# In an 8x8-state scan, TensorE adds ub to the second state by an identity product accumulated in its bank, and VectorE's order per step is changed

## The chip, the cores and the metric

One Trainium2 chip, one core. The metric is the device time in microseconds (us) of one execution, given as the median of several runs. The kernel runs a whole small network in one launch: a recurrent mixing layer with a time scan, followed by six layers of windowed attention and feed-forward. Only the scan is touched here.

## The reference, cut to what matters

```python
def step(s, inp):                      # s: one 8x8 state for each batch row and head
    q_, w_, k_, v_, a_, b_ = inp
    sa = jnp.einsum('bhij,bhj->bhi', s, a_)
    s = s * w_[:, :, None, :] + sa[..., None] * b_[:, :, None, :] + v_[..., None] * k_[:, :, None, :]
    return (s, jnp.einsum('bhij,bhj->bhi', s, q_))
s0 = jnp.zeros((Bx, H, HS, HS), x.dtype)       # H = 16 heads, HS = 8
_, y = jax.lax.scan(step, s0, (qt, wt, kt, vt, at, bt))      # B = 2, T = 1024
...
x = _layernorm(x + mixing(x));  x = _layernorm(x + six_layers(x))
```

Every token multiplies the state with `a`, sums over a head's 8 columns (`sa`), adds `sa * b` and `v * k`, and reads the state with `q`.

## The kernel before, in words

The 2 x 1024 tokens are cut into 64 chunks of 32 tokens, and all chunks run at once: a step `l` of the scan (`CHUNK` = 32 of them, l = 0 to 31) handles token l of every chunk. Since a chunk does not know its starting state, two states are carried. State 0 begins at zero and collects what the chunk adds (`v*k`). State 1 begins as the identity matrix and becomes the matrix that carries a starting state through the chunk. Each is a 128 x 512 fp32 tile in a PSUM bank of its own: `S_BANKS[0]` is bank 4, `S_BANKS[1]` is bank 5. Decays are folded into the step vectors, so a step only adds to a state. After the scan a serial chain over the 32 chunks of a sequence (`chain` on TensorE, `next_start` on VectorE) finds the starting states, then come the outputs of the mixing layer and the six layers (the "stream").

One step of the scan, for states p = 0 and 1:

- VectorE `times_a(p, l)` (L666): `m[p]` = state p times `a`.
- TensorE `product_u(p, l)` (L924): a product with `headones`, which sums over a head's rows, into `U_BANKS[p]`. A 128 x 512 fp32 product stands in the trace as two passes.
- VectorE `times_b(p, l)` (L671): `ub[p]` = that sum times `b`.
- State 1: VectorE `renew1(l)` (L684) adds `ub[1]` to bank 5 in place.
- State 0: GpSimd `add_vk(l)` (L845) makes `ubvk` = `ub[0]` + `vk`, and VectorE `renew0(l)` (L677) adds that to bank 4 in place.
- Reading: VectorE `times_r(l)` (L691) multiplies state 1 with `r`; ScalarE `copy_state(l)` (L514) copies bank 4 to SBUF and GpSimd `times_r(l)` (L852) multiplies the copy. TensorE `products_y(l)` (L932), 8 products of 128 columns in 16 passes, gathers both.
- GpSimd `times_k(l + 2)` (L838) prepares `vk` two steps ahead, from the tile `v_rep` that SyncE's copies (L453, 16 DMAs for 8 steps) fill.

Beside that, in steps 0 to 23, `in_step` inserts the making of the next group's step vectors: on VectorE two more instructions in the steps with l % 8 = 2, 3 and 4 and one with 5, 6 and 7 ("stages"); on TensorE `sums_of_squares` (L917) at l = 0, 8 and 16. TensorE also runs `product_rk` (L945) at l = 25 to 28.

The order on each engine is written out by hand, and every engine runs its own list in order. Per step TensorE's list is: `product_u(1, l+1)`, `product_u(0, l+1)`, `products_y(l-1)`, then `sums_of_squares` or `product_rk` if there is one. VectorE's is the loop at L732.

After the last step VectorE makes the first part of what the chain needs: `end_g` (L709, reads state 1), `spread_g_first` (L716), `make_prop` (L725), then `renew0(31)`, `times_r(31)`, `end_h` (L730) and two memsets (L752), on which the chain's first product waits.

Of the kernel before, what the change touches and what calls it, by code (L numbers as in the profile page):

```python
# [24 lines left out]
ALU = mybir.AluOpType  # L25
# [3 lines left out]
P = 128  # L29
B, T, C = 2, 1024, 128  # L30
N = B * T
HEADS, HS = 16, 8
GROUP = 512
GROUPS = N // GROUP
CHUNK = 32
CHUNKS = N // CHUNK
# [302 lines left out]
def build_steps(nc, a, sems, ctx, t, banks, v_dram, v_rep, state, y, zy, x_mid, x):  # L339


    def sig(name, **kw):
        return Signal(sems, name, **kw)

    def sb(name, shape):
        return ctx.enter_context(nc.sbuf_tensor(name, shape, F32))
# [9 lines left out]
    m, ub = sb("sc_m", [P, 2, W]), sb("sc_ub", [P, 2, W])  # L356
# [12 lines left out]
    s_set = sig("s_set")  # L369
    s_new = [sig(f"s_new{p}") for p in range(2)]  # L370
    s_a = [sig(f"s_a{p}") for p in range(2)]
    u_product = [sig(f"u_product{p}") for p in range(2)]
    ub_made = [sig(f"ub_made{p}") for p in range(2)]
    s_copied, y_product, y_read, ended = sig("s_copied"), sig("y_product"), sig("y_read", per=2), sig("scan_ended")
    s_r = [sig(f"s_r{p}") for p in range(2)]
# [8 lines left out]
    start = spare[:, CHUNKS * QUAD:CHUNKS * (QUAD + HS)].rearrange("p (c r) -> p c r", r=HS)  # L384
# [14 lines left out]
    U_BANKS, Y_BANKS, S_BANKS = (banks[0], banks[1]), (banks[2], banks[3]), (banks[4], banks[5])  # L399
# [7 lines left out]
    def step(tile, l):  # L407

        return tile[:, CHUNKS * l:CHUNKS * (l + 1)].unsqueeze(1).to_broadcast([P, HS, CHUNKS])

    def rows(ap):
        return ap.rearrange("p (r c) -> p r c", c=CHUNKS)
# [24 lines left out]
    def vk_of(l):  # L437
        return vk[(l // STEPS) % 2][:, :, l % STEPS, :]

    def in_step(l, stages):  # L440

        j, s = (l + STEPS) // STEPS, l % STEPS
        if j < GROUPS:
            for stage in stages[s]:
                stage(j)
# [158 lines left out]
    def vector(dve):  # L604
# [1 line left out]
        nc.vector.tensor_scalar(bonus_ones[:, :], t["headones"][:, :], vecs[:, V_FAAAA:V_FAAAA + 1], None, ALU.mult).then_inc(constants_made.sem, 1)  # L606
        nc.vector.scalar_tensor_tensor(out=head_centring[:, :], in0=t["headones"][:, :], scalar=-1.0 / HS, in1=t["ident"][:, :],
                                       op0=ALU.mult, op1=ALU.add).then_inc(constants_made.sem, 1)
        nc.vector.tensor_copy(rows(S_BANKS[1][:, :]), t["rowmask"][:, :].unsqueeze(2).to_broadcast([P, HS, CHUNKS])).then_inc(s_set.sem, 1)

        def soft_sum(j):
            dve.wait_ge(z_log.sem, j + 1)
# [44 lines left out]
        def times_a(p, l):  # L657

            if l:
                dve.wait_ge(s_new[p].sem, l)  # L660
            else:
                dve.wait_ge(s_set.sem, 1)
            if l >= 2 - p:
                dve.wait_ge(u_product[p].sem, l + p - 1)
            dve.wait_ge(a_made.sem, l // STEPS + 1)
            nc.vector.tensor_tensor(rows(m[:, p, :]), rows(S_BANKS[p][:, :]), step(a_step, l), ALU.mult).then_inc(s_a[p].sem, 1)  # L666

        def times_b(p, l):
            dve.wait_ge(u_product[p].sem, l + p)
            dve.wait_ge(b_made.sem, l // STEPS + 1)  # L670
            nc.vector.tensor_tensor(rows(ub[:, p, :]), rows(U_BANKS[p][:, :]), step(b_step, l), ALU.mult).then_inc(ub_made[p].sem, 1)  # L671

        def renew0(l):
            if l:
                dve.wait_ge(vk_added.sem, l + 1)
                dve.wait_ge(s_copied.sem, l)
                nc.vector.tensor_tensor(S_BANKS[0][:, :], S_BANKS[0][:, :], ubvk[:, :], ALU.add).then_inc(s_new[0].sem, 1)  # L677
            else:
                dve.wait_ge(vk_made.sem, 1)
                nc.vector.tensor_copy(rows(S_BANKS[0][:, :]), vk_of(0)).then_inc(s_new[0].sem, 1)  # L680

        def renew1(l):
            dve.wait_ge(ub_made[1].sem, l + 1)
            nc.vector.tensor_tensor(S_BANKS[1][:, :], S_BANKS[1][:, :], ub[:, 1, :], ALU.add).then_inc(s_new[1].sem, 1)  # L684

        def times_r(l):
            dve.wait_ge(s_new[1].sem, l + 1)
            dve.wait_ge(r_made.sem, l // STEPS + 1)
            if l >= 2:
                dve.wait_ge(y_product.sem, y_product.after(l - 2))  # L690
            nc.vector.tensor_tensor(m2[:, l % 2, :, 1, :], rows(S_BANKS[1][:, :]), step(r_step, l), ALU.mult).then_inc(s_r[1].sem, 1)  # L691
# [14 lines left out]
        def end_g():  # L706
            dve.wait_ge(s_new[1].sem, CHUNK)
            dve.wait_ge(ub_made[0].sem, CHUNK - 1)
            nc.vector.tensor_tensor(rows(G_BANK[:, :]), rows(S_BANKS[1][:, :]), last, ALU.mult).then_inc(g_set.sem, 1)  # L709
# [17 lines left out]
        def end_h():  # L727
            dve.wait_ge(s_copied.sem, CHUNK)
            dve.wait_ge(s_new[0].sem, CHUNK)
            nc.vector.tensor_tensor(rows(state[:, 0, :]), rows(S_BANKS[0][:, :]), last, ALU.mult).then_inc(ended.sem, 1)  # L730

        for l in range(CHUNK):  # L732
            if l:
                times_b(0, l)
            times_b(1, l)
            renew1(l)
            if l + 1 < CHUNK:
                times_a(1, l + 1)
            else:
                end_g()  # L740
                for s in range(B):
                    spread_g_first(s)
                for s in range(B):
                    make_prop(0, s)
            renew0(l)
            if l + 1 < CHUNK:
                times_a(0, l + 1)
            times_r(l)
            in_step(l, stages)
        end_h()  # L750
        for s in range(B):
            nc.vector.memset(start[:, SEQ_CHUNKS * s, :], 0.0).then_inc(start_set.sem, 1)  # L752
# [157 lines left out]
    def tensor(pe):  # L910

        def sums_of_squares(j):
            pe.wait_ge(squared.sem, j + 1)
            if j:
                pe.wait_ge(a_made.sem, j)
                pe.wait_ge(kk_gated.sem, j)
            nc.tensor.matmul(KK_BANK[:, :], t["headones"][:, :], sq[:, :], start=True, stop=True).then_inc(ss_product.sem, 1)  # L917

        def product_u(p, l):

            pe.wait_ge(s_a[p].sem, l + p)
            if l >= 2 - p:
                pe.wait_ge(ub_made[p].sem, l + p - 1)
            nc.tensor.matmul(U_BANKS[p][:, :], t["headones"][:, :], m[:, p, :], start=True, stop=True).then_inc(u_product[p].sem, 1)  # L924
# [11 lines left out]
        def product_rk(j):  # L936

            pe.wait_ge(rk_made.sem, j + 1)
            pe.wait_ge(constants_made.sem, 2)
            if j < 2:  # L940
                pe.wait_ge(r_made.sem, GROUPS)
                pe.wait_ge(kk_gated.sem, GROUPS)
            else:
                pe.wait_ge(rk_read.sem, j - 1)
            nc.tensor.matmul(RK_BANKS[j % 2][:, :], bonus_ones[:, :], rk[:, g_of[j]], start=True, stop=True).then_inc(rk_product.sem, 1)  # L945

        sums_of_squares(0)
        product_u(1, 0)
        stages = ((sums_of_squares,), (), (), (), (), (), (), ())
        for l in range(CHUNK):  # L950
            if l + 1 < CHUNK:
                product_u(1, l + 1)
                product_u(0, l + 1)
            if l:
                products_y(l - 1)
            in_step(l, stages)
            if l >= CHUNK - STEPS + 1 and l < CHUNK - STEPS + 1 + GROUPS:
                product_rk(l - (CHUNK - STEPS + 1))
# [1129 lines left out]
```

## Time and profile before

| | us |
|---|---|
| three runs | 1924.15, 1926.08, 1927.91 |
| median | 1926.08 |
| span of the profiled execution, first to last instruction | 1924.9 |
| scan in it, from the first `times_b` (L671) to the memset that lets the chain begin (L752) | 79.47 to 256.37 |

All times below are those of the profiled execution, counted from its first instruction. Its span is 1.2 us below the median of the runs. PE is the matmul row of TensorE and PEld its weight loads, DVE is VectorE, ACT is ScalarE, POOL is GpSimd. Neighbouring records of one kind are merged into one row with an "x" count; a record starts when its waits are over.

### The profile page before, as it was taken

The page shows a single profiled execution, that of the slowest core. Times are in us where ns is not written, and L with a number is a line of the kernel's source. Part 1 is how long each engine was busy: PE and PEld are TensorE (multiplying, and loading weights), DVE is VectorE, ACT ScalarE, POOL GpSimd, SP SyncE. Part 2 cuts the span into 40 slices and gives each one's busy share as a digit, 9 for nine tenths or more (in the row PEclk, how much of TensorE's full clock was granted, in tenths as well). Part 3 has the DMA queues.
Part 4 walks back from the last instruction along what each step waited for, and adds up shares of the span by engine and source line. Part 5 has one row for each costly group of instructions (what it writes and reads, how often), then busy time and mean ns, then how long its engine had stood idle before and what let it go on. Part 6 is the DMA issues. An engine that isn't in the chain of part 4 may idle for free.

```text
span 1924.9 us, 72907 instructions
## 1 busy us (share of the span) xinstructions
PE 1751.1 (91%) x31158; PEld 1185.3 (62%) x31158; DVE 1550.0 (81%) x2150; ACT 1138.0 (59%) x2221; POOL 1259.8 (65%) x981
## 2 busy tenths in 40 slices
PE   7577876899999989999899999899998999999985
PEld 2144553466666666667666767666666676666663
DVE  6599957788888878888888888788887888888853
ACT  5523223557676747676667676667675667676742
POOL 3476743777777767777667777677776777777730
PEclk9699977999999989999999999999998999999986
DMA  4534201222222232222322222322223222222220
GB/s 97 127 53 51 29 3 70 58 67 70 69 73 68 72 104 79 63 75 70 112 66 79 69 73 83 103 62 77 69 72 109 69 68 79 63 76 67 70 61 26
DMA packets 68257, 137.27 MB, mean 71 GB/s; under 512 B 17952, under 2 KB 23520, under 8 KB 66912
## 3 DMA queue, kind: packets, MB, share of 16 engines
q1 hardware_dynamic: 67936, 132.62, 27.0%
q8 instruction: 246, 4.03, 0.9%
q14 instruction: 75, 0.61, 0.1%
HBM read 29.79 MB, written 2.10 MB: 17 GB/s over the span
## 4 chain that ended last, share of the span: by engine, by line
PE 40%; DVE 22%; issue 11%; POOL 9%; DMA 7%; ACT 4%; SPq 2%; DVEq 0%; ACTq 0%; POOLq 0%
PE bank L1460 9%; PE bank L1370 6%; PE bank L1443 6%; POOL rot L1308 5%; DMA v_shift<-v_tok 5%; DVE rot L1770 5%; PE bank L1418 5%; PE bank L1501 3%; PE bank L1375 3%; PE bank L1477 3%; DVE total L1796 2%; DVE rnorm L1776 2%; POOL probs L1332 2%; DVE probs L1789 2%; DMA p_T<-p_blocks 1%
## 5 line engine op out<-in xcount | busy, mean ns | idle before, releaser
L1770 DVE TENSOR_TENSOR rot<-bank,gains 128x1024 f32<-128x1024 f32 x384 | 462.3, 1206 | 158.8 <-ACT squares L1603 142.8
L1314 POOL TENSOR_TENSOR rot<-rot,rnorm 128x1024 f32<-128x1024 f32 x192 | 361.0, 1901 | 319.3 <-ACT rnorm L1613 317.1
L1308 POOL TENSOR_TENSOR rot<-rot 128x512 f32<-128x512 f32 x384 | 480.6, 1274 | 6.9 <-DVE rot L1770 6.9
L1370 PE MATMUL bank<-wqkv,x 128*128 128x512 f32 x768 | 404.9, 612 | 10.5 <-issue 5.0
L1603 ACT ACTIVATE squares<-bank 128x512 f32<-128x512 f32 x384 | 232.8, 606 | 256.5 <-PE bank L1370 255.9
L1332 POOL TENSOR_TENSOR probs<-probs,total 128x1024 f32<-128x1024 f32 x96 | 182.7, 1903 | 125.3 <-DVE total L1798 125.3
L1644 ACT ACTIVATE o_T<-bank 128x512 f32<-128x512 f32 x192 | 104.2, 598 | 254.2 <-PE bank L1443 254.2
L1776 DVE TENSOR_REDUCE rnorm<-squares 128x16 f32<-128x1024 f32 x192 | 233.0, 1214 | 2.8
L1443 PE MATMUL bank<-p_T,v_shift 64*64 64x32 f32 x6144 | 194.7, 223 | 26.6 <-DMA p_T<-p_blocks 21.9
L1443 PEld LDWEIGHTS bank<-p_T,v_shift 64*64 64x64 f32 x6144 | 169.2, 138 | 79.1 <-issue 49.6
L1383 PEld LDWEIGHTS bank<-st_ident,rot 128*128 128x128 f32 x1536 | 179.9, 143 | 59.9 <-issue 53.6
L1375 PE MATMUL bank<-wqkv,x 128*128 128x512 f32 x384 | 206.6, 621 | 2.7 <-DVE rot L1770 2.7
L1443 PE MATMUL bank<-p_T,v_tok 64*64 64x32 f32 x6144 | 193.3, 222 | 4.4 <-issue 4.4
L1383 PE MATMUL bank<-st_ident,rot 128*128 128x128 f32 x1536 | 194.0, 275 | 0.0
L1460 PE MATMUL bank<-o_T,wo 128*128 128x256 f32 x768 | 176.9, 384 | 0.0
L1443 PEld LDWEIGHTS bank<-p_T,v_tok 64*64 64x64 f32 x6144 | 170.5, 139 | 5.5 <-issue 5.4
L1477 PE MATMUL bank<-xn_T,w 128*128 128x256 f32 (+1 forms) x576 | 164.5, 395 | 9.2 <-ACT gate_T L1670 2.2
L1460 PEld LDWEIGHTS bank<-o_T,wo 128*128 128x128 f32 x768 | 146.4, 192 | 42.9 <-issue 22.4
L1418 PE MATMUL bank<-k_T,q_T 64*32 64x64 f32 x12288 | 161.8, 225 | 11.8 <-issue 10.3
L1418 PEld LDWEIGHTS bank<-k_T,q_T 64*32 64x32 f32 x12288 | 140.8, 105 | 39.2 <-issue 33.1
L1477 PEld LDWEIGHTS bank<-xn_T,w 128*128 128x128 f32 (+1 forms) x576 | 97.7, 182 | 99.2 <-DVE ff_T L1822 45.5
L1370 PEld LDWEIGHTS bank<-wqkv,x 128*128 128x128 f32 x768 | 131.6, 191 | 39.1 <-issue 16.2
(196 smaller groups left out, 2849.2 us busy)
## 6 DMA issues: line engine op xcount, KB each, us to landing
p_T<-p_blocks SPq DMA_DIRECT2D x768, 64.0 KB
v_shift<-v_tok SPq DMA_DIRECT2D x96, 384.0 KB, 3.5
v_shift<-v_tok SPq DMA_DIRECT2D x96, 128.0 KB, 3.4
wqkv<-in_wqkv SPq DMA_DIRECT2D x6, 1536.0 KB, 8.0
v_rep_sb<-v_by_step SPq DMA_DIRECT2D x32, 128.0 KB
v_rep<-v_by_step SPq DMA_DIRECT2D x32, 128.0 KB
wo<-in_wo SPq DMA_DIRECT2D x6, 512.0 KB, 8.6
w<-in_w SPq DMA_DIRECT2D x6, 341.0 KB, 8.8
```

The source lines that it names most:

```text
L1308: nc.gpsimd.tensor_tensor(out=out, in0=out, in1=by_head(turned[:, part])[:, :, frm], op=ALU.add).then_inc(rot_added.sem, 1)
L1314: nc.gpsimd.tensor_tensor(out=by_head(qk[u][:, half]), in0=by_head(qk[u][:, half]), in1=rnorm[u][:, AH * i:AH * (i + 1)].unsqueeze(2).to_b ...
L1370: nc.tensor.matmul(QK_BANKS[i][:, :], shifted_tokens(x, n, P), layer_cols(wqkv, n, 3 * INNER, 512 * i, 512), start=True, stop=True).then_i ...
L1375: nc.tensor.matmul(V_BANKS[i][:, :], shifted_tokens(x, n, P), layer_cols(wqkv, n, 3 * INNER, 2 * INNER + 512 * i, 512), start=True, stop=T ...
L1383: mm = nc.tensor.transpose(outs[i // 4][:, P * (i % 4):P * (i % 4 + 1)], source[:, P * i:P * (i + 1)], ident[:, :])
L1418: mm = nc.tensor.matmul(s_banks(n)[p][at:at + WINDOW, 2 * WINDOW * a_:2 * WINDOW * (a_ + 1)], q_T[rows, a_, at:at + WINDOW], k_T[rows, a_, ...
L1443: mm = nc.tensor.matmul(o_banks(n)[g][DH * p:DH * (p + 1), at:at + WINDOW], v[rows, DH * head:DH * (head + 1)], p_T[n % 2][rows, turn_, he ...
L1460: mm = nc.tensor.matmul(ff_bank(m)[:, 0:PT], layer_cols(wo, n, INNER, C * i, C), o_T[:, i, :], start=(i == 0), stop=(i == PAIRS - 1))
L1477: mm = nc.tensor.matmul(ff_bank(m)[0:size, PT * j:PT * (j + 1)], layer_cols(w1, PAIR * m, 2 * FF, at + f0, size), xn_T[:, :], start=True, ...
L1603: nc.scalar.activation(squares[:, 512 * i:512 * (i + 1)], QK_BANKS[i][:, :], ACT.Square).then_inc(squared.sem, 1)
L1770: nc.vector.tensor_tensor(both, src.unsqueeze(1).to_broadcast([P, 2, 8, DH]), pair_of_gains.unsqueeze(2).to_broadcast([P, 2, 8, DH]), ALU. ...
L1776: nc.vector.reduce_sum(rnorm[n % 2][:, AH * h:AH * (h + 1)], by_head(squares[:, INNER * h:INNER * (h + 1)]), AX).then_inc(ss_made.sem, 1)
```

## The change

Four things change, all in the scan:

1. `renew1` leaves VectorE. TensorE does it with an identity product (`t["ident"]`, moving operand `ub[1]`) that accumulates in bank 5 (`start=False`). It stands first in TensorE's list of the step and waits for `ub[1]` of its step and for VectorE's `times_r(l-1)`, which reads the bank.
2. The initial state 1, an identity pattern that VectorE copied into the bank (L609), is put there by TensorE too, by an identity product of the row mask (`set_state`).
3. VectorE's order: `times_r` of a step moves behind `times_b(0)` of the next one, and state 0 is renewed and multiplied before state 1 is.
4. TensorE's `product_u(0)` now stands before `product_u(1)`.

```diff
-        nc.vector.tensor_copy(rows(S_BANKS[1][:, :]), t["rowmask"][:, :].unsqueeze(2).to_broadcast([P, HS, CHUNKS])).then_inc(s_set.sem, 1)
...
-        def renew1(l):
-            dve.wait_ge(ub_made[1].sem, l + 1)
-            nc.vector.tensor_tensor(S_BANKS[1][:, :], S_BANKS[1][:, :], ub[:, 1, :], ALU.add).then_inc(s_new[1].sem, 1)
...
         for l in range(CHUNK):
             if l:
                 times_b(0, l)
+                times_r(l - 1)
             times_b(1, l)
-            renew1(l)
+            renew0(l)
             if l + 1 < CHUNK:
+                times_a(0, l + 1)
                 times_a(1, l + 1)
             else:
                 end_g()
...
                 for s in range(B):
                     make_prop(0, s)
-            renew0(l)
-            if l + 1 < CHUNK:
-                times_a(0, l + 1)
-            times_r(l)
             in_step(l, stages)
+        times_r(CHUNK - 1)
         end_h()
...
+        def set_state():
+            nc.tensor.matmul(rows(S_BANKS[1][:, :]), t["ident"][:, :], t["rowmask"][:, :].unsqueeze(2).to_broadcast([P, HS, CHUNKS]),
+                             start=True, stop=False, skip_group_check=True).then_inc(s_set.sem, 1)
+
+        def renew1(l):
+            pe.wait_ge(ub_made[1].sem, l + 1)
+            if l:
+                pe.wait_ge(s_r[1].sem, l)
+            nc.tensor.matmul(S_BANKS[1][:, :], t["ident"][:, :], ub[:, 1, :], start=False, stop=True,
+                             skip_group_check=True).then_inc(s_new[1].sem, 1)
...
+        set_state()
         sums_of_squares(0)
         product_u(1, 0)
         stages = ((sums_of_squares,), (), (), (), (), (), (), ())
         for l in range(CHUNK):
+            renew1(l)
             if l + 1 < CHUNK:
+                product_u(0, l + 1)
                 product_u(1, l + 1)
-                product_u(0, l + 1)
             if l:
                 products_y(l - 1)
             in_step(l, stages)
```

VectorE's instructions of one step without stages, before (banks 0 and 1 hold the head sums of states 0 and 1; `s_new`, `ub_made`, `u_product` are raised by the renewals, `times_b` and `product_u`):

```order
L671 TENSOR_TENSOR sc_ub<-bank0,mk_sb 128x512 [waits b_step_made,u_product0]
L671 TENSOR_TENSOR sc_ub<-bank1,mk_sb 128x512 [waits b_step_made,u_product1]
L684 TENSOR_TENSOR bank5<-bank5,sc_ub 128x512 [waits ub_made1]
L666 TENSOR_TENSOR sc_m<-bank5,z_sb 128x512 [waits a_step_made,u_product1,s_new1]
L677 TENSOR_TENSOR bank4<-bank4,sc_ubvk 128x512 [waits s_copied,vk_added]
L666 TENSOR_TENSOR sc_m<-bank4,z_sb 128x512 [waits a_step_made,u_product0,s_new0]
L691 TENSOR_TENSOR sc_m2<-bank5,r_sb 128x8x64 [waits y_product,r_step_made,s_new1]
```

The same step of the changed kernel (its line numbers are 1 to 5 lower on VectorE):

```order
L670 TENSOR_TENSOR sc_ub<-bank0,mk_sb 128x512 [waits b_step_made,u_product0]
L686 TENSOR_TENSOR sc_m2<-bank5,r_sb 128x8x64 [waits y_product,r_step_made,s_new1]
L670 TENSOR_TENSOR sc_ub<-bank1,mk_sb 128x512 [waits b_step_made,u_product1]
L676 TENSOR_TENSOR bank4<-bank4,sc_ubvk 128x512 [waits s_copied,vk_added]
L665 TENSOR_TENSOR sc_m<-bank4,z_sb 128x512 [waits a_step_made,u_product0,s_new0]
L665 TENSOR_TENSOR sc_m<-bank5,z_sb 128x512 [waits a_step_made,u_product1,s_new1]
```

Seven instructions have become six: L684 is gone, the renewal of bank 4 follows at once on the second `times_b`, and `times_r` (of the step before) stands between the two `times_b`.

TensorE's list of one step, before:

```order
L924 MATMUL bank<-sc_m,headones_sb 128x512 [waits ub_made1,s_a1]
L924 MATMUL bank<-sc_m,headones_sb 128x512 [waits ub_made0,s_a0]
L932 MATMUL bank<-sc_m,collect_sb 128x128 [waits y_read,s_r1,s_r0]
L932 MATMUL bank<-sc_m,collect_sb 128x128 x7
```

And in the changed kernel, where `s_r1` is raised by VectorE's `times_r`:

```order
L921 MATMUL bank<-sc_ub,ident_sb 128x512 [waits s_r1,ub_made1]
L929 MATMUL bank<-sc_m,headones_sb 128x512 [waits ub_made0,s_a0]
L929 MATMUL bank<-sc_m,headones_sb 128x512 [waits ub_made1,s_a1]
L937 MATMUL bank<-sc_m,collect_sb 128x128 [waits y_read,s_r1,s_r0]
L937 MATMUL bank<-sc_m,collect_sb 128x128 x7
```

The renewal is a third 512-column product per step, ahead of the two others and behind the `products_y` of the step before.

## Rows read from the trace of the kernel before

**Rows 1.** The page, first part: busy us, share of the span, number of instructions
```profile
PE 1751.1 (91%) x31158; PEld 1185.3 (62%) x31158; DVE 1550.0 (81%) x2150; ACT 1138.0 (59%) x2221; POOL 1259.8 (65%) x981
```

**Rows 2.** Stretches: length, busy us per engine, granted TensorE clock, DMA share, GB/s
```profile
80.00:92.00 12.00, 8.35 (x13) 3.34 (x14) 8.27 (x14) 5.25 (x9) 5.00 (x4) 0.64 0.61 120
92.00:257.00 165.00, 128.02 (x639) 80.05 (x638) 153.97 (x245) 44.35 (x124) 115.34 (x94) 0.99 0.31 41
202.00:205.00 3.00, 3.00 (x15) 2.70 (x14) 2.41 (x5) 0.60 (x1) 1.69 (x2) 0.54 0.22 90
```

**Rows 3.** Timeline, all engines, one step: start, us, engine, line, operation [idle before <-releaser]
```profile
216.53 0.69 DVE L666 TENSOR_TENSOR sc_m<-bank,z_sb 128x512 f32<-128x512 f32 x1
217.14 0.68 DVE L691 TENSOR_TENSOR sc_m<-bank,r_sb 128x512 f32<-128x512 f32 x1
...
217.28 1.12 PE L924 MATMUL bank<-sc_m,headones_sb 128*128 128x512 f32 x2 [0.21 <-DVE sc_m L666]
...
218.24 1.95 PE L932 MATMUL bank<-sc_m,collect_sb 128*128 128x128 f32 x16
218.44 1.29 DVE L671 TENSOR_TENSOR sc_ub<-bank,mk_sb 128x512 f32<-128x512 f32 x2 [0.62 <-PE bank L924]
219.21 1.27 POOL L845 TENSOR_TENSOR sc_ubvk<-sc_ub,v_rep 128x512 f32<-128x512 f32 x1 [1.58 <-DVE sc_ub L671]
219.77 0.70 DVE L684 TENSOR_TENSOR bank<-bank,sc_ub 128x512 f32<-128x512 f32 x1
220.44 1.26 POOL L852 TENSOR_TENSOR sc_m<-sc_copy,r_sb 128x512 f32<-128x512 f32 x1
220.50 0.69 DVE L666 TENSOR_TENSOR sc_m<-bank,z_sb 128x512 f32<-128x512 f32 x1
221.11 0.69 DVE L677 TENSOR_TENSOR bank<-bank,sc_ubvk 128x512 f32<-128x512 f32 x1
221.67 1.27 POOL L838 TENSOR_TENSOR v_rep<-v_rep,k_sb 128x512 f32<-128x512 f32 x1
221.83 0.69 DVE L666 TENSOR_TENSOR sc_m<-bank,z_sb 128x512 f32<-128x512 f32 x1
```

**Rows 4.** Timeline, the next step: the gather and a 512-column product behind it
```profile
223.54 1.95 PE L932 MATMUL bank<-sc_m,collect_sb 128*128 128x128 f32 x16
223.74 1.29 DVE L671 TENSOR_TENSOR sc_ub<-bank,mk_sb 128x512 f32<-128x512 f32 x2 [0.62 <-PE bank L924]
225.33 1.02 PE L945 MATMUL bank<-kkraw_sb,bonus_ones 128*128 128x512 f32 x2
```

**Rows 5.** Chain that ended last, two steps with two stages each: start, us, what
```profile
147.14 1.29 DVE sc_ub L671 x2
152.92 1.29 DVE sc_ub L671 x2
```

**Rows 6.** Timeline, the scan's first steps
```profile
81.66 3.78 PE L924 MATMUL bank<-sc_m,headones_sb 128*128 128x512 f32 x4 [3.89 <-DVE sc_m L666]
91.73 1.29 DVE L671 TENSOR_TENSOR sc_ub<-bank,mk_sb 128x512 f32<-128x512 f32 x2 [1.57 <-PE bank L924]
```

**Rows 7.** Timeline, the last step and the start of the chain
```profile
250.24 1.29 DVE L671 TENSOR_TENSOR sc_ub<-bank,mk_sb 128x512 f32<-128x512 f32 x2 [0.62 <-PE bank L924]
...
252.24 1.26 POOL L852 TENSOR_TENSOR sc_m<-sc_copy,r_sb 128x512 f32<-128x512 f32 x1
252.30 0.70 DVE L709 TENSOR_TENSOR bank<-bank,decay 128x512 f32<-128x512 f32 x1
...
253.56 2.05 PE L932 MATMUL bank<-sc_m,collect_sb 128*128 128x128 f32 x16 [1.57 <-POOL sc_m L852]
...
256.37 0.08 DVE L752 MEMSET v_rep_sb<- 128x8 f32 x2
```

**Rows 8.** Timeline: the last copies into v_rep are issued, and GpSimd's first use of them
```profile
165.58 5.98 SPq L453 DMA_DIRECT2D v_rep<-v_by_step  x16
205.76 1.27 POOL L838 TENSOR_TENSOR v_rep<-v_rep,k_sb 128x512 f32<-128x512 f32 x1
```

## The prediction

> **What bounds the kernel now.** The page says PE 91%, DVE 81% [rows 1], but that is an average over stages; the change lives in the scan alone, so I read the scan by itself. From 92 to 257 us DVE is busy 153.97 of 165 us (93%), PE 128.02, POOL 115.34 [rows 2]: VectorE is the engine to look at. The timeline of one step without stages [rows 3, 4] shows why. `times_b(0)` starts at 218.44 and again at 223.74: a period of 5.30. In it VectorE runs seven instructions. One that does not need the one ahead starts 0.61 behind it (216.53 to 217.14), one that does 0.72 (221.11 to 221.83). The only gap is 0.62, ended by TensorE's L924. So before, a step is VectorE's seven instructions plus that short wait. Other steps: with two stages 5.78 (147.14 to 152.92) [rows 5], nine of them; one stage fits into the gap, so those nine take 5.30. The 29 periods from the `times_b(0)` at 91.73 to that of the last step at 250.24 are 158.5 us [rows 6, 7]; 9 x 5.78 + 20 x 5.30 = 158.0 agrees. Whatever leaves the scan leaves the total, since chain and stream follow serially.
>
> **Prices of what is added and moved.** All from [rows 3, 4, 7]. A 512-column product from standstill starts 0.06 after the VectorE instruction that releases it (216.53 + 0.69 to 217.28), takes 1.12 until its result and VectorE goes on 0.04 later (218.44); the array is free for the next work 0.96 after its start (218.24). With its weights loaded beforehand it takes 1.02 and occupies 0.86: the product at 225.33, straight behind a gather. The gather occupies 225.33 - 223.54 = 1.79. GpSimd's `add_vk` starts 0.77 after `times_b(0)` and takes 1.27; POOL releases another engine 0.06 after its end (252.24 + 1.26 to 253.56), and I take 0.05. GpSimd's three instructions need 3 x 1.23 = 3.7 per step.
>
> **The new step.** Set `times_b(0)` at 0. VectorE: `times_r` 0.61, `times_b(1)` 1.22. `renew0` could start at 1.94, but `ubvk` is ready at 0.77 + 1.27 + 0.05 = 2.09: the removed instruction uncovers a wait for GpSimd of 0.15 to 0.26. `times_a(0)` 2.81, its end 3.50, product 3.56, result and next `times_b(0)` at 3.56 + 1.12 + 0.04 = **4.72**. This is loop A, through VectorE, GpSimd, VectorE and TensorE.
> Loop B runs through TensorE's own list. From the array's start on `product_u(1)`: +0.86 the gather, +1.79 = 2.65 the identity product, +1.02 + 0.04 = 3.71 `times_a(1)`, +0.69 + 0.06 + 0.10 (weights) = **4.56**. B is 0.16 shorter than A, so A sets the step at 4.72 against 5.30. `times_a(1)` then starts near 3.5, when `times_a(0)` lets it go anyway (3.42): the identity product has next to no slack. That moving `renew1` costs the path nothing rests on this cover; whatever comes on top of it is paid once the 0.16 is used up.
>
> **The sum over the scan.**
> - Nine steps with one stage: the stage falls into VectorE's gap from 4.1 to 4.72. 9 x (4.72 - 5.30) = -5.2.
> - Nine with two: VectorE runs without a gap, 3.42 + 3 x 0.61 = 5.25. 9 x (5.25 - 5.78) = -4.8.
> - Five plain ones (l = 8, 16, 24, 25, 30): -2.9.
> - Where `sums_of_squares` stands behind the gather, the identity product starts 0.86 later, `times_a(1)` at 4.37, and `product_u(0)` is pushed too: the step takes 5.2 (l = 9, 17), -0.2, and passes 0.3 on to the next one each, +0.6.
> - `product_rk` in four successive steps: the first 5.2, then loop B with 0.86 more, 5.42, three times: -0.1 + 0.4 = +0.3. Here the new kernel is slower than the old one.
> - Start: TensorE is at the lower of its two levels for much of 80 to 92 us (granted 0.64), a product pair taking some 1.9 (3.78 for two) [rows 2, 6]. In step 0 `renew1` is on TensorE at that price, but the two head sums now begin early; I get `times_b(0)` of step 2 at 89.0 instead of 91.73, then a step of 6.9 if the clock is low for a stretch of it, as the granted share for 80 to 92 has it: 1.6 more than its 5.25. Net -1.1.
> - One stretch of 3.4 us at the lower level near 202 [rows 2] cost the old kernel 0.4, hidden mostly; with TensorE in both loops it costs 1.4: +1.0.
> - End: `end_g` waits for TensorE's last renewal, at 3.51 after `times_b(0)` instead of 2.06 (252.30 - 250.24); `renew0` has left the list behind it (-0.6). The memset that lets the chain begin comes at 6.9 to 7.0 instead of 6.13 (256.37 - 250.24) [rows 7]: +0.8.
> - `set_state` runs at the start while ScalarE works toward the first `sums_of_squares`; the VectorE copy that it replaces stood in a wait for ScalarE. Nothing either way, at most 0.1.
> - SyncE's queue: the last copies into `v_rep` are issued at 165.58, and GpSimd wants them at 205.76 [rows 8]. Both move with the scan, but the seven steps between are 3.3 us shorter. The copies' end is not shown by a row to the tenth, only that traffic is low from 202 on (share 0.22) [rows 2]. So 0 to 1.5 us of wait on GpSimd, which has 1.0 of slack per step; I take 0.
> Sum -5.2 - 4.8 - 2.9 - 0.2 + 0.6 + 0.3 - 1.1 + 1.0 + 0.8 = **-11.5 us**. From the profiled span of 1924.9 that is 1913.4; with the 1.2 us by which the median stands above it, 1926.1 - 11.5 = **1914.6**.
>
> **What is not in the trace of before: an accumulating identity product and a weight load behind a fresh wait.** Accumulation: seven of a gather's eight products accumulate, and 1.79 / 16 = 0.112 a pass gives no sign of a price; the lower bound is 0, the upper one rival 3's. The weight load: at 225.33 it was hidden under the gather, at 217.28 it was exposed (1.12 against 1.02). In a plain step `ub[1]` is ready at 1.96, the array free at 2.45, so I take it hidden; exposed, it costs 0.10 at the head of loop B in every step without cover and the sum falls to -9.4.
> The Trainium skill, "TensorE: Matmul & The Clock Gate", in its part on the architectural detail, says that TensorE pulls weight loads ahead of running matmuls. By that rule the load is hidden as I take it; by the exposed row the total would be 1916.7.
>
> **Rivals.**
> 1. *The result of the identity product is late* (exposed weights, a slower turn between TensorE and VectorE, GpSimd's sum coming later). Loop B has 0.16 of slack in plain steps, some 0.5 in two-stage ones, none in the `product_rk` steps. Walking the steps with 0.2 us more gives -7.9, with 0.4 -3.6, and the gain is gone at 0.57. Against it: every latency is from rows of the same engines. Time 1918 to 1922.5.
> 2. *TensorE's clock.* Between 80 and 92 us and near 202 us the low level struck the old kernel although TensorE was working [rows 2]. If the busier TensorE escapes both stretches, 1.6 and 1.0 to 1.4 come back: -14.3, 1911.8. The Trainium skill, the same page, Part 1 on the warmup, says that the throttled state is the default and that activity releases it; by that rule this is the outcome. The trace speaks half against it: the low stretch at 202 came in dense work. If instead further low stretches come, each costs 1.7 us.
> 3. *The other side: accumulating into a bank that another engine reads and that already holds data runs at half rate at 512 columns.* Then the identity product occupies 1.71, loop B is 4.56 + 0.85 = 5.41 in plain steps against 5.30, and 6.27 in `product_rk` steps. Over the scan I get +11: 1937. It is slower than before from about 0.57 us of additional time per product. Against it speaks the gather's pitch of 0.112 per accumulating pass; for it only that no 512-column product accumulates in this scan.
> 4. *Nothing gained:* VectorE's freed 0.7 us is replaced by waits of the same size, so that the step stays near 5.2. It takes the same 0.4 to 0.6 us as in rival 1: 1922 to 1930.
>
> **How the numbers follow.** Forecast -8 to -14 (1912 to 1918): 0.70. Rival 1, 1918 to 1922.2: 0.11. Rival 2, 1910 to 1912: 0.07. Rival 4 within 0.2%: 0.06. Rival 3 and the slow end of 4: 0.06. A change of 0.2% (3.9 us) is about what a measurement of this kernel can tell from none. So faster 0.88, same 0.06, slower 0.06. The range 1910 to 1921 holds the forecast, rival 2 and most of rival 1.
>
> **What would show it.** Right: `times_b(0)` to `times_b(0)` 4.7 in plain and one-stage steps, 5.25 in two-stage, 5.4 in three of the `product_rk` steps; VectorE waiting 0.15 to 0.26 for GpSimd's `add_vk` before each `renew0` of a plain step; PE pairs of 1.02 straight behind the gather; `end_g` 3.5 behind its step's `times_b(0)`. Wrong: a step above 4.9 with VectorE idle before `times_a(1)`, or PE idle between the gather and the identity product; a gap on GpSimd before `times_k(24)`. The forecast fails if loop B, not A, sets the plain step, or if the clock is low for more than two stretches of the scan.

## The result, and the profile after

| us | kernel before | changed kernel |
|---|---|---|
| median of the runs of the comparison | 1925.12 (4 runs) | 1905.55 (1897.81 to 1908.25, 4 runs) |
| span of the profiled execution | 1924.9 | 1906.3 |
| scan in it, first `times_b` to the memset ahead of the chain | 176.9 | 161.6 |
| from that memset to the end | 1668.5 | 1665.2 |

The ratio is 0.9896, 95% interval [0.9871, 0.9921]. One later execution of the kernel before took 4243 us, more than twice as long as any other, and is left out of every figure. Forecast were 1914.6 and a range of 1910 to 1921: faster, as said, but by some 20 us and not by 11.5. The time lies below the range. Two different things were missed, and the table shows both: the scan lost 15.3 us, and behind the scan, where nothing was changed, time went as well: 3.3 us in this pair of executions, 5.6 as a mean over many (below).

First the step. The timeline of the changed kernel, one plain step, answers to [rows 3, 4] (start, duration, engine, line and operation, idle before it and what ended that):

```profile
200.70 0.70 DVE L676 TENSOR_TENSOR bank<-bank,sc_ubvk 128x512 f32<-128x512 f32 x1 [0.18 <-POOL sc_ubvk L839]
200.96 0.30 PEld L921 LDWEIGHTS bank<-sc_ub,ident_sb 128*128 128x128 f32 x2
201.07 1.02 PE L921 MATMUL bank<-sc_ub,ident_sb 128*128 128x512 f32 x2
201.43 1.39 DVE L665 TENSOR_TENSOR sc_m<-bank,z_sb 128x512 f32<-128x512 f32 x2
202.18 1.98 PE L929 MATMUL bank<-sc_m,headones_sb 128*128 128x512 f32 x4
203.34 0.69 DVE L670 TENSOR_TENSOR sc_ub<-bank,mk_sb 128x512 f32<-128x512 f32 x1 [0.52 <-PE bank L929]
203.95 0.68 DVE L686 TENSOR_TENSOR sc_m<-bank,r_sb 128x512 f32<-128x512 f32 x1
204.00 1.95 PE L937 MATMUL bank<-sc_m,collect_sb 128*128 128x128 f32 x16
204.11 1.28 POOL L839 TENSOR_TENSOR sc_ubvk<-sc_ub,v_rep 128x512 f32<-128x512 f32 x1 [0.98 <-DVE sc_ub L670]
204.55 0.68 DVE L670 TENSOR_TENSOR sc_ub<-bank,mk_sb 128x512 f32<-128x512 f32 x1
205.42 0.70 DVE L676 TENSOR_TENSOR bank<-bank,sc_ubvk 128x512 f32<-128x512 f32 x1 [0.20 <-POOL sc_ubvk L839]
205.68 0.30 PEld L921 LDWEIGHTS bank<-sc_ub,ident_sb 128*128 128x128 f32 x2
205.78 1.02 PE L921 MATMUL bank<-sc_ub,ident_sb 128*128 128x512 f32 x2
```

From L676 to L676 it is 205.42 - 200.70 = 4.72, the forecast period. `add_vk` starts 0.77 after `times_b(0)` (203.34, 204.11), `renew0` waits 0.20 for it, and the identity product takes 1.02, its weights loaded beforehand (PEld 205.68, PE 205.78). The two `times_a` are one row of 1.39, where two instructions that wait for nothing take 1.29 (218.44 in [rows 3]). So `times_a(1)` is held for 0.10 by the identity product, whose result is there at 201.07 + 1.02 = 202.09, and starts 3.5 behind `times_b(0)`, as forecast. That costs the step nothing, since on TensorE `product_u(1)` stands behind `product_u(0)` anyway (202.18, both in one row of 1.98).

Then TensorE's clock and load by stretches. The rows of windows give: stretch, its length, then busy us of PE, PEld, DVE, ACT and POOL with their instruction counts, granted clock, DMA share, GB/s. The changed kernel, from 80 us to the end of its scan:

```profile
80.00:92.00 12.00, 11.61 (x32) 5.40 (x32) 8.98 (x15) 5.14 (x9) 7.43 (x6) 0.78 0.61 116
92.00:241.00 149.00, 142.01 (x667) 86.97 (x666) 131.85 (x208) 44.30 (x124) 112.63 (x92) 1.00 0.33 45
```

Against [rows 2] the clock is higher in the first stretch (0.78 for 0.64), and from 92 us on it is 1.00: no stretch at the lower level at all. The forecast had two such stretches in it.

The waits of VectorE between 84 and 242 us (what waited, for what: us in total, times, longest):

```profile
DVE sc_m L665 <- PE bank L921: 6.3, 9, 1.1
DVE bank L676 <- POOL sc_ubvk L839: 5.8, 30, 0.2
DVE sc_ub L670 <- PE bank L929: 5.3, 14, 1.0
```

Thirty times 0.2 for GpSimd, as forecast. For the identity product VectorE shows nine waits of its own, all in the steps that also hold a `sums_of_squares` or a `product_rk` or follow on one.

### The profile page after: what moved, and what is told of

It is laid out like the page before. It is cut to its first block, busy times and chain, and to the rows that moved or that the text cites. A ratio compares the mean times of both kernels' runs of the same rounds, so it can differ in the third digit from the quotient of the medians.

```text
span 1906.3 us, 73037 instructions
## 1 busy us (share of the span) xinstructions
PE 1774.9 (93%) x31224; PEld 1201.0 (63%) x31224; DVE 1527.7 (80%) x2117; ACT 1138.3 (60%) x2221; POOL 1260.5 (66%) x981
## 4 chain that ended last, share of the span: by engine, by line
PE 42%; DVE 16%; POOL 10%; issue 10%; DMA 10%; ACT 4%; SPq 4%; DVEq 0%; POOLq 0%; ACTq 0%
PE bank L1467 9%; PE bank L1450 7%; PE bank L1377 6%; POOL rot L1315 5%; DMA v_shift<-v_tok 5%; DVE rot L1777 5%; PE bank L1425 5%; PE bank L1382 3%; PE bank L1508 3%; PE bank L1484 3%; DVE rnorm L1783 2%; DVE total L1803 2%; POOL probs L1339 2%; DVE probs L1796 2%; PE bank L1390 2%
## 5 line engine op out<-in xcount | busy, mean ns | idle before, releaser
L1450 PE MATMUL bank<-p_T,v_shift 64*64 64x32 f32 x6144 | 197.9, 225 | 31.9 <-DMA p_T<-p_blocks 31.6
```

The lines of the kernel that those rows point to most:

```text
L1450: mm = nc.tensor.matmul(o_banks(n)[g][DH * p:DH * (p + 1), at:at + WINDOW], v[rows, DH * head:DH * (head + 1)], p_T[n % 2][rows, turn_, he ...
```

## Experiments

`times_b(0)` to `times_b(0)` is the period of a step. "Behind" is the time from the memset ahead of the chain to the end; where it is called a mean, it is the mean span of all runs of a kernel less the scan of its trace and less 79.4 us for what stands ahead of the scan (78.3 to 79.6 in the traces), and the value of before beside it is that of the runs taken together with them. The low time is the time in an execution at TensorE's lower level (1.2 GHz), worked out from the mean granted clock that each run has.

### The changed kernel again

> The changed kernel once more, for more times and a second profile. Theory: its gain is the scan's, 15 to 16 us from the first times_b to the memset before the chain (161.6 us after, 176.9 before), and what stands behind the scan differs between runs by several us either way through the granted clock. So the scan part reads 161 to 164 us, the part behind it lies anywhere in 1660 to 1672, and the ratio over five rounds settles near 1 - 15.3/1925 = 0.992 (0.990 to 0.994). Rival: the change also shortens what follows the scan, by some 5 us in every run; then the ratio stays at 0.9895 or lower and the part behind the scan reads below 1665 again.

Measured: 1906.70 (6 runs), ratio 0.9903 [0.9879, 0.9928]; behind, 1663.8 as a mean against 1667.4 of before (18 runs). Scan 162.6, one us more than in the first trace. Its timeline shows why, in the step at 113.44:

```profile
114.04 1.28 POOL L832 TENSOR_TENSOR v_rep<-v_rep,k_sb 128x512 f32<-128x512 f32 x1 [2.05 <-DMA v_rep<-v_by_step]
115.26 1.28 POOL L839 TENSOR_TENSOR sc_ubvk<-sc_ub,v_rep_sb 128x512 f32<-128x512 f32 x1
116.57 0.70 DVE L676 TENSOR_TENSOR bank<-bank,sc_ubvk 128x512 f32<-128x512 f32 x1 [1.25 <-POOL sc_ubvk L839]
```

GpSimd waits 2.05 us for the copies into `v_rep`, its sum comes late, VectorE waits 1.25 for it where 0.20 is usual. That is the DMA term, which I had bounded at 0 to 1.5 and taken as 0. It exists, costs 1.05 us here, and comes at the second group of steps, not at the last as I had placed it. It differs between executions: in the same step GpSimd waits 1.50 us in the third trace of the changed kernel (the step takes 5.22) and 1.85 with the five added products below (5.58), and the first trace shows 4.72 there.

### One half of the change at a time

The first kernel keeps the identity product and takes back the two orders:

```diff
             if l:
                 times_b(0, l)
-                times_r(l - 1)
             times_b(1, l)
-            renew0(l)
             if l + 1 < CHUNK:
-                times_a(0, l + 1)
                 times_a(1, l + 1)
...
+            renew0(l)
+            if l + 1 < CHUNK:
+                times_a(0, l + 1)
+            times_r(l)
             in_step(l, stages)
...
             renew1(l)
             if l + 1 < CHUNK:
-                product_u(0, l + 1)
                 product_u(1, l + 1)
+                product_u(0, l + 1)
```

> The identity product on TensorE as in the change, but VectorE and TensorE keep the order of before (state 1 first, times_r last, product_u(1) ahead). Theory of two loops: times_a(1) now waits for a product that stands behind the gather on TensorE, and everything of state 0 queues behind it on VectorE; a plain step takes 5.87 us (before 5.30), a two-stage step 6.26, a product_rk step 6.72, the scan 198 us, 21 more than before: 1946. Rival: the gain comes from taking an instruction off VectorE, in whatever order; then this is as fast as the change, plain step 4.7.

The second keeps the order of the changed kernel, with `renew1` on VectorE behind `times_b(1)` and no identity product.

> The new order on VectorE and TensorE, but renew1 stays on VectorE, ahead of renew0 (seven instructions a step, no identity product). Theory of two loops: a plain step is 1.9 (times_b, times_r, times_b) + 0.7 renew1 + 0.7 renew0 + 0.7 times_a + 1.2 product = 5.15 to 5.2 us, two-stage 5.7, product_rk steps 5.15 like the plain ones; scan 171 to 173, 4 to 6 less than before, about 1921. With the run before it the two do not add up to the change (+21 and -5 against -15): each half needs the other. Rival: the order is what gains, then this lies within 3 us of the change.

Measured. The move alone: 1940.89 (5 runs), ratio 1.0079 [1.0053, 1.0105]; scan 198.8, plain steps 5.88, two-stage 6.23, `product_rk` steps 6.75. The order alone: 1921.88 (10 runs), ratio 0.998 [0.9962, 0.9998]; scan 174.45, plain steps 5.16, two-stage 5.64, with four stretches of 3.4 us at the lower level in it (the first at 89.0). VectorE of the move alone, around 205 us:

```profile
202.80 1.28 DVE L670 TENSOR_TENSOR sc_ub<-bank,mk_sb 128x512 f32<-128x512 f32 x2
205.30 0.69 DVE L665 TENSOR_TENSOR sc_m<-bank,z_sb 128x512 f32<-128x512 f32 x1 [1.22 <-PE bank L921]
209.03 1.28 DVE L670 TENSOR_TENSOR sc_ub<-bank,mk_sb 128x512 f32<-128x512 f32 x2
```

VectorE stands still for 1.22 us between the second `times_b` and `times_a(1)`, until the identity product has put the state there. So here, giving the instruction away makes the scan 21.9 us longer when nothing stands in that gap. In the changed kernel `renew0` and `times_a(0)` fill it. The order alone takes 2.5 us from the scan, both together 15.3. Of the order's own gain, some 2.4 us more are hidden by its three low stretches behind 93 us (six periods stand above their like, as 5.68 for 5.16 and 6.13 for 5.64), so the order is worth nearer 5 than 2.5 at an undisturbed clock.

### The identity product twice as long

```diff
+            nc.tensor.matmul(S_BANKS[1][:, :], no_ident[:, :], ub[:, 1, :], start=False, stop=True, skip_group_check=True)
```

A second accumulating product, of a matrix of zeros, stands behind each identity product.

> The change with a second product per renewal, with all-zero weights, accumulated into the same bank (adds nothing, 0.86 us more on TensorE). Theory: loop B (product_u(1), gather, identity product, times_a(1)) was only 0.16 shorter than loop A, so 0.7 of the 0.86 is paid in plain steps: 5.40 in place of 4.72; two-stage 5.8, product_rk steps 6.26; scan 184 in place of 161.6, total about 1928. Rival: TensorE has slack in the scan and the step is VectorE's; then the plain step stays under 4.9.

Measured: 1926.54 (1 run), scan 184.2; plain steps 5.41, two-stage 5.77, `product_rk` steps 6.27. The product adds 0.86 to TensorE's list and the plain step grows by 5.41 - 4.72 = 0.69. What lies between is the slack of loop B, 0.17 (0.16 by the forecast), so loop A sets the step of the changed kernel and B is right behind it. The step is B's 4.56 + 0.86 = 5.42. TensorE's rows of one step, the identity product, the one of zeros and the head sums:

```profile
206.13 1.02 PE L923 MATMUL bank<-sc_ub,ident_sb 128*128 128x512 f32 x2
206.99 1.02 PE L924 MATMUL bank<-sc_ub,no_ident 128*128 128x512 f32 x2
207.85 2.07 PE L932 MATMUL bank<-sc_m,headones_sb 128*128 128x512 f32 x4
```

The accumulating products start 0.86 apart and take 1.02 each, as the product that starts a bank does (225.33 in [rows 4]). A bank that already holds data makes no difference.

### Products that nobody waits for, in the kernel before

This is the test of what the forecast took for granted, that behind the scan nothing moves. The kernel before gets one more product ahead of each gather, into the bank that the gather overwrites. It falls into TensorE's idle time.

```diff
             pe.wait_ge(y_read.sem, y_read.after(l - 2))
+            nc.tensor.matmul(Y_BANKS[l % 2][:, :], t["ident"][:, :], t["collect"][:, 0:GROUP], start=True, stop=True)
             for i in range(HS):
```

> The kernel before with one more 512-column product per step on TensorE, of constant tiles, put ahead of the gather into the gather's bank, where the gather's first product overwrites it; nobody waits for it and VectorE's order is the old one. TensorE is then as busy in the scan as in the change. It asks whether the 4 to 6 us that all three kernels with identity products gained behind the scan (and the absence of low clock stretches in their scans) come from TensorE's activity. Activity theory: no stretch at the lower clock from 92 us on in the scan, scan 175 to 176, the part behind it 1661 to 1666 in place of 1668.5, total 1919 to 1921. Rival, that it has to do with where the scan ends or with chance: scan 176 to 177, behind it 1667 to 1670, total as before, 1925. If the old loop does not have the room on TensorE that I read (0.86 us between the gather and product_u(1)), plain steps rise above 5.30.

> The kernel before once more, for a second profile. Under the activity theory its scan again has one or more stretches of 3.4 us at the lower clock after 92 us (0.4 to 1 us each), scan 176.5 to 178.5, and the part behind it reads 1667 to 1672. Under chance the two readings scatter as widely as those of the changed kernels, 1661 to 1674.

Measured: 1919.57 (10 runs) against 1928.48 (15 runs of before), ratio 0.9956 [0.994, 0.9972]. The kernel before as a control, unchanged: 1926.0 (1 run), scan 176.9. With the products the steps are the old ones (5.29 plain, 5.78 two-stage) and the scan takes 176.2. Yet the whole is 8.6 us shorter as a mean (1917.7 against 1926.3): behind, 1662.1 against 1670.0. The scan, first row before and second row with the products, then 96 us of the chain and what follows it in the same order:

```profile
92.00:250.00 158.00, 123.51 (x591) 76.10 (x591) 147.72 (x230) 42.63 (x118) 111.61 (x90) 0.99 0.32 42
```

```profile
92.00:250.00 158.00, 144.55 (x654) 86.69 (x653) 147.98 (x231) 42.64 (x118) 111.93 (x91) 1.00 0.31 42
```

```profile
257.00:353.00 96.00, 68.26 (x1272) 41.06 (x1273) 57.12 (x164) 34.00 (x67) 39.37 (x44) 0.75 0.12 42
```

```profile
257.00:353.00 96.00, 70.45 (x1390) 42.50 (x1387) 61.32 (x167) 37.34 (x74) 43.95 (x46) 0.79 0.14 46
```

The same 96 us hold more work of every engine (VectorE 61.32 for 57.12) at a granted clock of 0.79 instead of 0.75. Part of that is that the memset came 1.2 us earlier (255.19, 256.37), at most 1.2 us of the 4.2. In its second trace the kernel before has 55.66 and 0.72. The low time of a whole execution falls from 169 to 146 us as a mean.

### Halving two instructions of loop A

`times_b(0)` and `add_vk` are cut into two instructions of four rows each, so that GpSimd can begin after the first half.

> The change with times_b(0) and GpSimd's add_vk each cut into two instructions of four rows, so that GpSimd starts on the first half while VectorE makes the second. It shortens loop A alone. Theory: ubvk is ready some 0.25 us earlier, VectorE's own order then sets renew0 at 1.98, and the plain step falls to 4.60 (loop B stands at 4.56); two-stage steps grow by the extra instruction to 5.26; product_rk steps stay at 5.41; scan about 1 us shorter or equal, total within 0.1% of the change. Rival: loop A is not what sets the plain step; then it stays at 4.72 or grows.

Measured: 1910.59 (4 runs), 0.9912 [0.9891, 0.9932]; scan 162.0, plain period 4.74 (203.35 to 208.09). VectorE and GpSimd of one step:

```profile
203.35 0.76 DVE L674 TENSOR_TENSOR sc_ub<-bank,mk_sb 128x256 f32<-128x256 f32 x2 [0.54 <-PE bank L940]
203.94 1.42 POOL L849 TENSOR_TENSOR sc_ubvk<-sc_ub,v_rep 128x256 f32<-128x256 f32 x2 [0.87 <-DVE sc_ub L674]
204.62 0.68 DVE L677 TENSOR_TENSOR sc_ub<-bank,mk_sb 128x512 f32<-128x512 f32 x1
205.45 0.70 DVE L684 TENSOR_TENSOR bank<-bank,sc_ubvk 128x512 f32<-128x512 f32 x1
```

GpSimd starts 0.59 after `times_b(0)` and not 0.77, but its two halves take 1.42 and not 1.27. They end at 2.01 (2.05 before, 204.11 + 1.28 - 203.34). `renew0` follows at 2.10 against 2.08, so nothing was gained. Loop A was not shortened, and how much loop B would leave of a shorter one is not shown by this run.

### Filling the changed kernel too

```diff
+        filler(CHAIN_BANKS[0])
+        filler(CHAIN_BANKS[0])
...
         def last_y(i):
```

`filler` is a product of the identity with a constant that nobody reads. Two of them stand between the end of the scan and the chain.

> The changed kernel beside the two that follow, on the same chip. Scan 161.6 to 162.7 us (the larger if the copies into v_rep land late as in the second profile); the part behind it 1661 to 1667; ratio to before 0.989 to 0.991.

> The change with only the two products ahead of the chain. Activity theory: the first low stretch behind the scan begins 4 us or more after the chain's start in place of 1.1, the gather products woven into the chain take 0.71 in place of 1.16 to 1.22 a pair, the chain ends 2 to 3 us earlier. Rival: the low stretch begins within 2 us of the chain's start as in the change.

The third kernel has three more such products between the first head sums, where TensorE waits before the scan.

> The change with five more 512-column products on TensorE that nobody waits for: three while the scan is being prepared (one each is some 1.7 us at the lower clock) and two between the last gather of the scan's loop and the chain, where the changed kernel's TensorE stands idle for 1.6 us and its clock falls 1.1 us after the chain begins (242.2). Activity theory: the clock is high from about 75 us on, so the first two steps lose 1 to 1.5 us (scan 160.3 to 161), and it stays high into the chain, whose 31 steps take 30 us in the kernels where it did and 33 in this one: 2 to 3 us less behind the scan; total 1902 to 1904, ratio 0.987 to 0.989. Rival: the clock falls in the chain whatever stands before it, and the gains seen behind the scan were chance or came from the position: total as the change, within 1 us.

Measured: the changed kernel 1904.53 (6 runs), 0.9889 [0.9863, 0.9914]; with the two products 1907.05 (4 runs), 0.9885 [0.986, 0.9911]; with all five 1903.11 (5 runs), 0.9879 [0.9852, 0.9906]. The three can't be told apart. TensorE in the chain, with the two products:

```profile
243.53 0.71 PE L979 MATMUL bank<-sc_m,collect_sb 128*128 128x128 f32 x4
244.17 0.31 PE L988 MATMUL bank<-v_rep_sb 32*32 32x8 f32 x16
```

In the changed kernel itself, at the same place:

```profile
243.20 0.40 PE L982 MATMUL bank<-v_rep_sb 32*32 32x8 f32 x16
243.53 1.22 PE L973 MATMUL bank<-sc_m,collect_sb 128*128 128x128 f32 x4
```

A group of four products takes 0.71 at the higher level and 1.22 at the lower one. The first low stretch begins 7.1 us after the memset with the two products and 1.1 to 3.0 without, the chain takes 30.8 us instead of 31.6 to 33.1. That much was bought, and the total shows nothing of it beyond its scatter. The products ahead of the scan moved a low stretch (to 80.6 us) and shortened the first period from 4.55 to 4.18; the wait for the copies (0.86 in that execution) took more than that, so that this scan takes 162.05.

### Where that activity has to be

Two more variants of the kernel before. One has two such products only, in TensorE's two waits ahead of the chain. The other has the product ahead of the gathers of steps 0 to 23 only (`if l < 24`).

> The kernel before with two products that nobody waits for, one in each of TensorE's two waits ahead of the chain (1.57 us before the last gather, 0.89 behind it). Steps and scan as before, 176 to 177 us. Theory 'the clock at the chain's start is what the added TensorE work in the scan buys': the first stretch at the lower level begins 6 to 7 us behind the memset instead of 2.8 to 3.0, the chain takes 30 to 31.5 us instead of 33 to 35, and the whole is as with a product in every step: 0.9945 to 0.997 of before, 4 to 8 us behind the scan. Theory 'it takes the activity of the whole scan': the chain may gain 1 to 2 us, the total at most 0.1%, 0.999 to 1.000.

> The kernel before with one product that nobody waits for ahead of each gather of steps 0 to 23 only, none in the last eight steps. Steps and scan as before, 176 to 177 us, with no stretch at the lower level before step 24 and possibly one behind it. Theory 'the clock at the chain's start, that is the last steps, is what counts': nothing is gained, 0.999 to 1.000 of before, the chain 33 to 35 us. Theory 'activity of the whole scan counts': some three quarters of the gain of a product in every step, 0.996 to 0.998, 3 to 6 us behind the scan.

Measured: the two late products, 1927.09 (12 runs) against 1926.45 (17), ratio 1.001 [0.9999, 1.0021]. The early ones, 1919.69 (5 runs), ratio 0.9961 [0.9948, 0.9973], scan 176.4, behind 1661.9 as a mean against 1667.6. The last TensorE rows of the scan, first with the late products:

```profile
253.44 2.05 PE L932 MATMUL bank<-sc_m,collect_sb 128*128 128x128 f32 x16 [0.71 <-POOL sc_m L852]
255.33 1.02 PE L963 MATMUL bank<-collect_sb,ident_sb 128*128 128x512 f32 x2
256.37 0.99 PE L980 MATMUL bank<-v_rep_sb 32*32 32x8 f32 x32
```

Then with the early ones:

```profile
253.20 2.05 PE L934 MATMUL bank<-sc_m,collect_sb 128*128 128x128 f32 x16 [1.57 <-POOL sc_m L852]
256.13 1.00 PE L977 MATMUL bank<-v_rep_sb 32*32 32x8 f32 x32 [0.88 <-DVE v_rep_sb L752]
```

The kernel whose TensorE goes busy into the chain gains nothing; the one that has the old waits of 1.57 and 0.88 there, but was busy in steps 0 to 23, gains 0.39%. The theory that the clock at the chain's start is what the added activity buys, which I held when I filled the changed kernel, is refuted for the kernel before.

## Why the prediction was wrong

**Right, by its own steps.** The mechanism and nearly every duration. Loop A sets the plain step at 4.72 (4.72 measured); `product_rk` steps 5.2, 5.42, 5.42, 5.42 (5.22, 5.41, 5.41, 5.41); the step with `sums_of_squares` 5.2 (5.22) and 0.3 passed on (5.50 for 5.20); 0.15 to 0.26 of wait for GpSimd (0.18 to 0.20); the weights hidden in plain steps (in two-stage steps the identity product takes up to 1.12, where loop B has room); the end 0.8 later (0.7: 241.07 - 234.24 = 6.83 against 6.13). Rival 1 (a late product) and rival 4 (nothing gained) did not occur, and rival 3 (half rate) is refuted by the rows of 1.02 and by the doubled product. Two sums of the working do not follow from its own slack of 0.16, which the doubled product confirmed (0.17). An exposed weight load of 0.10 leaves loop B at 4.66, still below 4.72, so it would have cost under 1 us in the steps without slack and not the 2.1 behind -9.4. And 0.2 more in loop B would have cost some 2.2, not the 3.6 behind rival 1's -7.9.

**Wrong inside the scan, 3.8 us.** The sum gave -11.5, measured are -15.3:
- The low stretch in step 2 (+1.6) did not come. That step took 5.31, not 6.9, as the rows of its two `times_b(0)` show (the second with `times_b` of the last step and the memset below it):

```profile
88.78 0.69 DVE L670 TENSOR_TENSOR sc_ub<-bank,mk_sb 128x512 f32<-128x512 f32 x1 [0.62 <-PE bank L929]
...
94.09 0.68 DVE L670 TENSOR_TENSOR sc_ub<-bank,mk_sb 128x512 f32<-128x512 f32 x1
...
234.24 0.69 DVE L670 TENSOR_TENSOR sc_ub<-bank,mk_sb 128x512 f32<-128x512 f32 x1 [0.33 <-PE bank L929]
...
241.07 0.08 DVE L746 MEMSET v_rep_sb<- 128x8 f32 x2
```

- The low stretch near 202 (+1.0) did not come either, and the 0.5 that it cost the old kernel (5.78 for 5.30 in that step) went too: 1.5. So the part of the result inside the scan is rival 2, which had a chance of 0.07 and said -14.3. Low stretches that begin in the scan behind 93 us stand in three of the eleven kernels: before (PE busy for 123.51 of 158 us), the order alone (118.49 of 155, three of them) and the one with two late products (124.68 of 158). These are the three with no product added in steps 0 to 30. The eight that have one in the steps, be it the identity product or one that nobody waits for, have no such stretch. The Trainium skill, "TensorE: Matmul & The Clock Gate", Part 1 on the warmup, says that the throttled state is the default and that activity releases it; for the scan the traces agree. I argued against it from the one low stretch that fell into dense work, but over the whole scan TensorE was busy for 123.51 of 158 us only, and the change made it 142.01 of 149. The step that failed is to carry a clock over from the old profile into a stretch whose TensorE load the change raises.
- Two-stage steps are 5.20 and not 5.25: 0.45. Start and end: 0.3.

**Wrong behind the scan, 5.6 us.** The sentence that failed is "Whatever leaves the scan leaves the total". 16 runs of the changed kernel have a mean span of 1904.5, 60 of the kernel before 1924.8: 20.3 us, of which the scan is 14.8 (three traces). The rest, 5.6, was gained in code that is the same instruction for instruction (up to 0.4 of it may lie ahead of the scan, which starts at 79.0 as a mean instead of 79.4). One comparison differs from the next: 4.6, 3.6 and 6.8 us. No term, no rival and no bound of the range had it. That added TensorE products in the scan can do this without shortening it is shown, by those that nobody waits for (7.9 behind an almost unchanged scan) and by those in steps 0 to 23 alone (5.7). That it is their activity, and not the 24 or 31 more instructions in TensorE's list, is the likelier reading and not shown: every kernel that gained has both, and none was run with as many added instructions that leave TensorE idle. The move alone shows it in a kernel that is slower as a whole (1660.7 behind). The order alone, without further activity, has 1666.1 against 1667.4.

Over 131 runs, compared within each kernel, a run's span falls by 0.27 us (standard error 0.03) for each us less of low time, and this explains half of the scatter. If this slope held between kernels too, the 23 us by which the products lowered it would make 6 of the 8.6. For the changed kernel the low time falls from 168 to 155 us, but in its three traces 10 to 14 of these lie ahead of the memset; behind it they have 135 to 145 us against 129 and 132 of before. So its gain behind the scan is not fewer low stretches in sum, and that they lie at better places is only an inference.

**What stays open.** Where the gain sits: up to the 33rd of the 384 `squares` of the stream, 178 us behind the memset, the traces of the changed kernel are 3.6 to 6.3 us ahead of before, those with the added products 7.5 (steps 0 to 23) and 8.0, the one with two late products 1.3 behind. Then the middle layers give it back (at the 353rd the changed kernel stands between 2.1 ahead and 0.8 behind, the two with added products at 2.0 ahead and 0.6 behind), and the last stretch brings some again. The low stretches there come once per layer, 3 to 16 us of them, at its boundary. I found no rule by which activity in the scan acts up to 200 us later, and none for the giving back. The kernel with the halves has the same TensorE load as the changed kernel and gains 2.4 us behind the scan (1667.6 as a mean of 4 runs against 1670.0 of before): the least of the kernels with added products, but with a standard error of 1.5 it does not contradict the 3.6 of the changed kernel's second comparison, and at the 33rd `squares` its trace is 3.7 ahead, like the changed kernel's.

## What to carry to other kernels

Where an instruction is handed to an idle engine, fill the gap that it leaves with work that doesn't need its result: here the same move costs 22 us of scan or, with the order changed, gains 15. Two loops worked out from rows of the old trace (this one 4.72 and 4.56) gave the new period to the hundredth in plain steps (4.72) and to 0.05 in two-stage ones. And when a change raises or lowers TensorE's load, don't carry the clock of the old profile over, neither in the stretch itself nor behind it, and don't count on "what leaves this stage leaves the total": widen the range to the side to which the activity goes.

## What the runs showed of the hardware that I had not expected

- 24 products of 0.86 us that nobody reads, in a stretch whose length stays the same within 0.7 us (176.4 for 176.9), make the program 0.39% shorter (0.9961 [0.9948, 0.9973]), and 31 of them 0.44% (0.9956 [0.994, 0.9972]). Two of them right ahead of a serial chain do nothing (1.001 [0.9999, 1.0021]), although they put off its first low stretch from 3.0 to 5.8 us behind the memset.
- An accumulating 128 x 512 product into a bank that VectorE reads and that holds data takes 1.02, as one that starts a bank does.
- Two GpSimd additions of half a tile take 1.42 where one of the whole takes 1.27.
